# Attention kernel on one Trainium2 core: each DMA transpose of the softmax probabilities is split in two

## The reference, cut to what matters

```python
xn = _layernorm(x)
q = jnp.einsum('bpd,hde->bphe', xn, W_Q) + b_Q          # k and v likewise
scores = jnp.einsum('bqhe,bkhe->bhqk', q, k) / sqrt(128)
scores = jnp.where(causal, scores, -100000.0)
attn = jax.nn.softmax(scores, axis=-1)
z = jnp.einsum('bkhe,bhqk->bqhe', v, attn)
s = jnp.einsum('bqhe,hed->bqd', z, W_O) + b_O
g = silu(ffn(xn))                                       # gate, up and down weights
out = x + s * g
```

## Time and profile before

| | |
|---|---|
| median of 3 runs | 1094.77 us (1092.81 to 1095.11) |
| the profiled execution | 1092.56 us, of which the span in the trace is 1090.8 us |
| granted TensorE clock | 1.00 over the span |
| PE busy | 1064.8 us, 98% of the span |
| DVE, ACT, POOL busy | 810.0, 736.0, 196.0 us |
| DMA queue q1 | 295872 packets, 179.64 MB, 66.4% of 16 engines |
| probability transposes | 128, 1291 to 4103 ns each on SP's queue, 3.9 to 7.6 us from issue to landing |

### The profile page before, as it was taken

One profiled execution on the slowest core, in us unless ns is written; L12 is line 12 of the kernel. 1 busy time (PEld: TensorE's weight loads), 2 busy tenths in 40 slices (PEclk: granted clock), 3 DMA queues, 4 the chain that ended last, 5 costly groups with the idle time before them and its releaser, 6 DMA issues.

```text
span 1090.8 us, 21485 instructions
## 1 busy us (share of the span) xinstructions
PE 1064.8 (98%) x7452; PEld 705.2 (65%) x7452; DVE 810.0 (74%) x2005; ACT 736.0 (67%) x1832; POOL 196.0 (18%) x195
## 2 busy tenths in 40 slices
PE   6999999999899999999999999999999999999998
PEld 3444444446667777777777777777777777777764
DVE  7776877786777777777777777777777777777876
ACT  6855556656677777767777776777766666666662
POOL 1000201012101121122312212132000001144434
PEclk9999999999999999999999999999999999999999
DMA  7436666677777769788896897879667667868866
GB/s 267 150 77 167 161 194 188 189 245 201 157 209 208 179 166 263 173 187 208 227 233 168 210 232 164 214 175 266 163 132 198 141 144 177 233 165 232 216 163 172
DMA packets 318532, 207.66 MB, mean 190 GB/s; under 512 B 251872, under 2 KB 284640, under 8 KB 317920
## 3 DMA queue, kind: packets, MB, share of 16 engines
q1 hardware_dynamic: 295872, 179.64, 66.4%
q10 hardware_dynamic: 19200, 15.73, 4.6%
q0 software_dynamic: 3360, 11.01, 2.8%
HBM read 109.87 MB, written 34.60 MB: 132 GB/s over the span
## 4 chain that ended last, share of the span: by engine, by line
PE 80%; ACT 7%; DMA 5%; DVE 5%; issue 2%; SPq 0%; ACTq 0%; DVEq 0%
PE bank L729 71%; PE bank L911 8%; ACT arena L1277 2%; DMA split_v<-w_out 2%; DMA XT<-V 1%; DMA split_qk<-w_out 1%; ACT w_out L1113 1%; ACT arena L1291 1%; DVE arena L1367 1%; DMA arena<-arena 1%; ACT V L1138 1%; DVE arena L1489 1%; DVE w_out L1383 0%; DMA arena<-x_dram 0%; DVE bank L1643 0%
## 5 line engine op out<-in xcount | busy, mean ns | idle before, releaser
L729 PE MATMUL bank<-XT,arena 128*128 128x256 f16 (+2 forms) x1872 | 311.1, 314 | 2.8 <-DMA XT<-V 1.5
L729 PE MATMUL bank<-arena 128*128 128x512 f16 (+1 forms) x1124 | 269.2, 379 | 0.2 <-issue 0.2
L729 PEld LDWEIGHTS bank<-XT,arena 128*128 128x128 f16 (+1 forms) x1872 | 179.2, 98 | 112.5 <-issue 7.9
L1277 ACT ACTIVATE arena<-bank,neg_max 128x512 f32<-128x512 f32 (+3 forms) x256 | 132.6, 524 | 139.0 <-DVE neg_max L1643 139.0
L729 PE MATMUL bank<-ST,arena 128*128 128x256 f16 x1536 | 199.4, 273 | 1.3 <-DVE arena L1585 0.5
L729 PEld LDWEIGHTS bank<-arena 128*128 128x128 f16 x1124 | 109.6, 98 | 107.6 <-issue 0.9
L729 PEld LDWEIGHTS bank<-ST,arena 128*128 128x128 f16 x1536 | 148.0, 98 | 25.6 <-ACT arena L1234 3.3
L1660 DVE SCALAR_TENSOR_TENSOR arena<-arena,inv_sum 128x512 f16<-128x512 f32 (+3 forms) x256 | 127.2, 559 | 9.5 <-ACT arena L1291 7.3
L1643 DVE CUSTOM_DVE_ANT_0 bank<-bank,mask 128x512 f32<-128x512 f32 (+3 forms) x256 | 118.0, 517 | 21.6 <-PE bank L729 21.4
L1291 ACT ACTIVATE arena<-arena,inv_sum 128x512 f16<-128x512 f32 (+3 forms) x256 | 122.4, 557 | 0.0
L911 PE MATMUL bank<-arena,V 128*128 128x512 f16 x756 | 113.0, 299 | 1.8 <-issue 0.9
(11 more groups left out here) (124 smaller groups left out, 1560.5 us busy)
## 6 DMA issues: line engine op xcount, KB each, us to landing
arena<-split_qk SPq DMA_DIRECT2D x64, 896.0 KB, 5.3
w_in<-attn_w_dram SPq DMA_DIRECT2D x64, 256.0 KB, 4.0
split_qk<-w_out ACTq DMA_DIRECT2D x28, 256.0 KB, 3.8
arena<-ffn_w_dram SPq DMA_DIRECT2D x8, 768.0 KB, 4.7
arena<-x_dram SPq DMA_DIRECT2D x20, 256.0 KB, 4.1
parked_silu<-arena ACTq DMA_DIRECT2D x4, 1024.0 KB, 4.5
arena<-split_o SPq DMA_DIRECT2D x4, 1024.0 KB, 6.6
split_qk<-w_out SPq DMA_DIRECT2D x13, 256.0 KB, 3.3
```

What stands on the lines that cost most here:

```text
L729: mm = nc.tensor.matmul(out, stationary(a, k), moving(b, k), start=first and n == 0 and i == 0, stop=last and n == len(tiles) - 1 and i == ...
L1277: e = nc.scalar.activation(probs[:, at:at + width], SC[b_][:, col:col + width], ACT.Exp, bias=neg_max[:, i:i + 1], scale=-1.0, accum_out=r ...
```

## The change

Each of the two transposes of a unit is issued as two: first places 0 to 6 (key tiles 0 and 1), then places 8 to 12 (key tiles 2 and 3 with the two gaps between them). The gap at place 7 is no longer transposed. So there are four transposes to a unit, of 7, 5, 7 and 5 blocks, in place of two of 13 blocks. Both halves of a part count on the same semaphore, and everyone who waits for a part waits for both of its halves: the values waited for are doubled by `PT_TURNS`.

```diff
@@ -95,6 +95,8 @@
 GAPS = [(7, 1), (10, 2)]
+KEY_BLOCKS = [(0, 7), (8, 13)]
+PT_TURNS = 16 * len(KEY_BLOCKS)
 PW = 1280
@@ -554,8 +556,10 @@
                 for part, split in ((0, p_hi), (1, p_lo)):
                     sp.wait_ge(split, TT * (n + 1))
 
-                    sp.dma_start_transpose(out=PT[part], in_=P_SPLIT[part].rearrange("p b k -> p (b k)")
-                                           ).then_inc(pt_ok[part], 16)
+                    for lo, hi in KEY_BLOCKS:
+                        sp.dma_start_transpose(out=PT[part][:, lo:hi],
+                                               in_=P_SPLIT[part][:, lo:hi].rearrange("p b k -> p (b k)")
+                                               ).then_inc(pt_ok[part], 16)
@@ -911,11 +915,11 @@
-                pe.wait_ge(pt_ok[0], 16 * (u + 1))
+                pe.wait_ge(pt_ok[0], PT_TURNS * (u + 1))
                 for j in range(TT):
                     part(0, 0, j, first=j == 0)
                     part(1, 0, j)
-                pe.wait_ge(pt_ok[1], 16 * (u + 1))
+                pe.wait_ge(pt_ok[1], PT_TURNS * (u + 1))
@@ -1283,7 +1287,7 @@
-                    act.wait_ge(pt_ok[0], 16 * n)
+                    act.wait_ge(pt_ok[0], PT_TURNS * n)
@@ -1653,7 +1657,7 @@
-                    dve.wait_ge(pt_ok[1], 16 * n)
+                    dve.wait_ge(pt_ok[1], PT_TURNS * n)
```

## The result

| | kernel before | changed kernel |
|---|---|---|
| median of the runs | 1094.1 us (1092.81 to 1095.11, 4 runs) | 1102.93 us (1100.9 to 1104.38, 4 runs) |
| ratio to before, 95% interval | | 1.0082 (1.0069 to 1.0095) |
| the profiled execution, its span | 1092.56, 1090.8 us | 1103.97, 1102.2 us |

The changed kernel is slower by 0.82%, 8.8 us between the medians and 11.4 us between the two profiled executions. The predicted 1094.7 us is wrong, and the time lies above the range, which ended at 1098.8.

What follows compares the result with a forecast made beforehand. PE was taken to bound the attention (busy 99.79 of 100 us). Ordinary units 0, units 13, 37 and 61 -0.1 each at best, the end -0.1: -0.2 to 0 from the median 1094.77, so 1094.7 us; range 1092.4 to 1098.8.

Steps and rivals of the forecast that it cites:

- the slope: SP's transpose issues: length follows the blocks, 0.14 us each, so 7 blocks cost 0.65 us and 5 cost 0.4.
- break-even of 1.03 us: SP's queue: issue length, (5.8 - 2.7) / 3, at which the low part would land as late as before.
- the rival: SP's four issues set the pace at a fixed 1.3 to 1.5 us each: 1098.6 to 1102.6 us, chance 0.2.
- The 1317 ns: One issue of 16 blocks on SP, as short as the shortest of 13; would suit a fixed price of 1.3.
- the 1291 ns: Shortest issue of 13 blocks on SP in the profile before; typical was 1.49 us as first of a pair.
- Cover of ordinary units: Low part lands 3.5 us (unit 34) or 2.8 us (unit 35) before PE's weighing needs it.
- the landing of a small transpose: DMA of 5 blocks: lands 1.9 + 0.8 = 2.7 us after its own issue.
- the last landing by the rival: Low part lands 6.7 to 7.2 us after the unit's first issue against 5.8, so 0.9 to 1.4 late.
- SP's slack: SP's queue: transposes hold it 3.49 us, 6.1 at 1.5 us an issue; its 5.9 us wait a unit hides that.
- the places without cover: Units 13, 37, 61 and 63 expose lateness in full, units 1 and 3 only above 0.8 us.
- the second rival: Neighbouring transposes don't overlap: 11.4 us in place of 5.8, PE waits in each unit, some 1250 us, chance 0.01.
- The rival's sum: Four exposed places 3.6 to 5.6, units 1 and 3 0.2 to 1.2, unit 13 up to 1 more: 3.8 to 7.8 us.

Runs made afterwards that it cites:

- the first halves alone: Kernel before with only places 0 to 6 of each part transposed, key tiles 2 and 3 not at all: 1091.65 us against 1093.11, one run.
- k_hi: Kernel before, two whole transposes, the low part's issue held back until ACT wrote the high part of the next keys' second half: 1097.08 us, 1.0051.
- the burst later: Changed kernel with SP's weight traffic of units 13, 29 and 45 issued behind the transposes: 1098.96 us, 1.0057.

## Why the prediction was wrong

*What failed: the length of a small issue.* The step is "I take the slope, three cases against one". It read 0.14 us a block from issues of 13 and 16 blocks and carried the line down to 7 and 5. The slope is real up there, but it ends at a floor: 1.28 us for 7 and 5 blocks, 1.23 for one. By the prediction's own break-even of 1.03 us the rival was true at once. The 1317 ns and the 1291 ns of the earlier trace rows lay just above that floor, in plain sight: the shortest issues of 13 and of 16 blocks were the same, and that is what a fixed price looks like. Two sizes close together can't show a floor below both; the minimum of each can hint at it.

*Right: the parts around it.* Cover of ordinary units (the lag grows by no more than 0.12 us in 52 of 64 units); the landing of a small transpose (2.7 by the sum, 2.65 measured); the last landing by the rival (6.7 by the sum, 6.57 in an undisturbed unit, 6.99 in the median); SP's slack (6.1 us by the rival at most, 5.2 in the median, no wait from it in an ordinary unit); and the places without cover that it listed, 1, 3, 13, 37, 61 and 63, which all paid, though 51 was not among them. Four transposes overlap, so the second rival was false: the four land 1.0 to 1.8 us apart. Nothing was to be gained, as the first halves alone show.

*The rival's sum.* It had 3.8 to 7.8 us; its places took 7.1 in the profile (0.21 + 0.67 + 2.18 + 0.40 + 1.82 + 1.79, units 1 and 3 less what units 2 and 4 gave back). That this fits is partly luck: with POOL held back unit 61 takes nothing and the end 0.63. SP's lateness in unit 13 was given up to 1 us and is 2.0. Two terms were missing. POOL's transfers now meet the last transpose in units 51, 61 and 63: with them held back the median is 5 us lower. And behind unit 13's wait of 1.95 us the clock went down: 1.7 us more, by the estimate above. The late output weights, 0.8 us, were missing as well, since I looked only at the head weights behind the transposes.

*Weights of the cases.* A single number, the issue's length, carried both cases, and the evidence for it was read on one side only; 0.75 against 0.2 was too sure, and a range that ended at the low end of the rival's left most of it out.

The advice of the Trainium skill ("DMA: Bandwidth & Descriptors", rules for kernel authors) to coalesce small transfers was right here, but not by the fixed 2.0 us that the page puts on each DMA of the software issued path (anatomy of one DMA): here what an issue spends beside its data overlaps, the landings of the four being 1.0 to 1.8 us apart. Against another sentence of that page (Issuing engines are not separate DMA queues), by which the time to initiate a DMA "is usually small relative to the DMA itself", the measurement decides: 1.28 us of SP's queue for 7 blocks that flow in 1.1 us (7 x 0.157).

## What to carry to other kernels

Split a DMA only when its issue is known to be shorter than the data of a piece. For the DMA transposes here the issue alone took 1.2 to 1.3 us for 1 to 7 blocks of 32 KB, more than the 1.1 us in which 7 blocks flow, so with small pieces the issues set the pace: the last landing came at 5.89 us with two pieces, 6.99 with four and 11.92 with eight. To find such a floor, compare the shortest issues of different sizes, not the typical ones. And when something lands later, ask what else will be on the DMA engines then: here the transfers of POOL that were met there made about half of the loss.

## What the runs showed of the hardware

- An issue of a DMA transpose between two places of SBUF, median: 1.23 us for one block of 128 x 128 float16, 1.21 to 1.30 for 2 to 7, 1.5 for 13, 1.9 for 16; right behind 13 blocks 1.72 for 7 and 1.97 for 13.
- A transpose issued just ahead of a store or load of 256 KB by POOL landed 3.9 us (unit 63), 5.0 us (unit 61) and 5.3 us (unit 51) after its issue, undisturbed 2.65; with POOL's transfers held back 2.7 in all three.
- After PE had been idle for 1.95 us (unit 13) and for 2.35 us (the end with `k_hi`) the granted clock fell to 0.50 for 3.4 us; the first of these cost some 1.7 us beyond the wait. Behind the waits of 1.2 us (unit 51), 1.6 us (unit 61 and the end) and 1.86 us (unit 51 with the burst later) the granted clock stayed at 1.00.
